# One core, attention and routed experts: the end of the first attention in another order

## What is computed

```python
x = x + attn_a(layernorm(x))     # qkv, windows of 64 with 16 heads of 8, projection,
                                 # + residual; layer norm, 128->512 GELU, 512->128, + residual
x = x + ffn(layernorm(x))        # router: top 2 of 8 experts; silu(x W1[e]) W2[e], gated
x = x + attn_b(layernorm(x))     # overlapping windows of 128, one softmax over all 128 features
x = x + ffn(layernorm(x))
```

## Time and profile before

| | |
|---|---|
| median of 3 runs | 621.07 us (612.94 to 622.57) |
| profiled execution | 618.1 us, span 616.2 us |
| mean granted PE clock | 0.881 of full speed |
| PE busy | 476.2 us, 77% of the span |
| DVE busy | 314.9 us, 51% |
| POOL busy | 251.7 us, 41% |
| ACT busy | 233.3 us, 38% |
| chain that ended last | PE 64%, DVE 15%, issue 8%, DMA 5%, POOL 3%, ACT 2% |

### The profile page before, as it was taken

How to read it: one execution, slowest core, us unless ns; L and a number is a source line. 1 busy time by engine, 2 the same in 40 slices (tenths; PEclk the granted TensorE clock), 3 DMA queues, 4 the chain that set the end, 5 groups by cost and what they waited for, 6 DMA issues and landing times.

```text
span 616.2 us, 12385 instructions
## 1 busy us (share of the span) xinstructions
PE 476.2 (77%) x3973; PEld 375.2 (61%) x3995; DVE 314.9 (51%) x1032; ACT 233.3 (38%) x483; POOL 251.7 (41%) x233
## 2 busy tenths in 40 slices
PE   1839999999989999766977999138776399599940
PEld 1525676867767786736867777116565287577730
DVE  5545586858876897745401010086977442010105
ACT  6715556474546447041321222114542022122320
POOL 7033343334342654435173533421265607533440
PEclk9957899999989999867997999658996589799985
DMA  7581092873748180012113200220010311320006
GB/s 256 184 186 31 20 192 60 155 155 64 161 72 158 34 173 14 14 35 70 33 57 86 69 15 27 64 90 1 0 36 26 75 41 50 87 66 31 24 23 204
DMA packets 66401, 48.35 MB, mean 78 GB/s; under 512 B 7669, under 2 KB 60423, under 8 KB 66342
## 3 DMA queue, kind: packets, MB, share of 16 engines
q1 hardware_dynamic: 61238, 36.99, 27.1%
q0 software_dynamic: 5104, 10.57, 4.8%
HBM read 16.14 MB, written 27.59 MB: 71 GB/s over the span
## 4 chain that ended last, share of the span: by engine, by line
PE 64%; DVE 15%; issue 8%; DMA 5%; POOL 3%; ACT 2%; SPq 2%; POOLq 0%; DVEq 0%; ACTq 0%
PE PS L796 12%; PE PS L656 8%; PE PS L780 7%; PE PS L782 4%; PE PS L643 3%; PE PS L781 3%; PE PS L701 3%; PE PS L618 3%; PE PS L600 3%; PE PS L708 2%; PE PS L559 2%; DVE X L1678 2%; PE PS L759 2%; PE PS L666 2%; PE PS L627 2%
## 5 line engine op out<-in xcount | busy, mean ns | idle before, releaser
L497 POOL DMA_INDIRECT YY<-W2R,ID x78 | 76.4, 980 | 85.7 <-ACT W2R L1230 65.6
L441 POOL TENSOR_TENSOR R<-NM,I64B 128x1024 bf16<-128x1024 f32 x32 | 61.5, 1922 | 112.9 <-DVE NM L1371 107.9
L1222 ACT ACTIVATE W2R<-PS 128x512 f32<-128x512 f32 x78 | 46.6, 597 | 160.4 <-PE PS L782 160.3
L796 PE MATMUL PS<-WB,W2R 128*128 x624 | 92.5, 295 | 0.0
L1638 DVE COPY QKM<-PS 128x1024 bf16<-128x1024 bf16 (+1 forms) x20 | 13.6, 678 | 148.0 <-PE PS L759 148.0
L483 POOL DMA_INDIRECT XS<-W1R,SLOT x64 | 63.4, 990 | 57.8 <-PE PS L782 33.4
L780 PE MATMUL PS<-QKM,WA 128*128 128x128 bf16 x312 | 71.7, 234 | 12.1 <-DVE QKM L1638 4.5
L796 PEld LDWEIGHTS PS<-WB,W2R 128*128 128x128 f32 x624 | 79.7, 200 | 1.7 <-issue 0.2
L782 PE MATMUL PS<-QKM,WA 128*128 128x128 bf16 x312 | 71.8, 234 | 0.0
L781 PE MATMUL PS<-QKM,WA 128*128 128x128 bf16 x312 | 69.7, 227 | 0.0
L656 PEld LDWEIGHTS PS<-VB,PF 128*128 128x128 f32 x512 | 59.6, 191 | 6.3 <-issue 6.3
(11 more groups left out here) (197 smaller groups left out, 864.9 us busy)
## 6 DMA issues: line engine op xcount, KB each, us to landing
XS<-CST SPq DMA_DIRECT2D x30, 520.0 KB, 9.1
QKM<-XS SPq DMA_DIRECT2D x78, 65.0 KB
QKM<-QK SPq DMA_DIRECT2D x64, 72.0 KB, 2.1
QKM<-YY SPq DMA_DIRECT2D x8, 512.0 KB, 5.7
W2R<-in_W POOLq DMA_DIRECT2D x1, 2048.0 KB, 11.5
YY<-W2R,ID POOLq DMA_INDIRECT x78, 2.2
XS<-CST SPq DMA_DIRECT2D x2, 585.0 KB, 9.2
XS<-W1R,SLOT POOLq DMA_INDIRECT x64, 2.4
```

What stands on the lines that cost most here:

```text
L441: nc.gpsimd.tensor_tensor(R[:, u % 2], NM[:, u % 2].unsqueeze(2).to_broadcast([P, NH, WIN]), I64B[:].unsqueeze(1).to_broadcast([P, NH, WIN ...
L497: pool.indirect_dma_start(out=YY[f], out_offset=to, in_=YS[n % NY][:, i, :], in_offset=None, bounds_check=NPAIRS - 1, oob_is_err=False) \
L796: last = mm(o, HF[n % 3][:, k, :], WB[:, e, k, :].rearrange("p o c -> p (o c)"), start=k == 0, stop=k == KF - 1)
L1222: fn(HF[n % 3], PS[:, n % 3, :].rearrange("p (k s) -> p k s", k=KF), ACT.Silu).then_inc(s["f_hf"], 1)
```

## The change

At the end of the first attention the order on every engine is another. The last unit of attention (context 31) is freed of `output_a(2)` and of the first table. Then come, on PE, `project(3)`, `output_a(2)`, `h_t(3)`, the four hidden matmuls of batch 3 in four banks (5, 0, 1, 2), a new `output_a_by_quarter(3)`, which takes each hidden quarter as its GELU is done, and only then `route_x_t(0, 2)` and `logits(0, 2)`. Batch 1's logits, choice, ranks and place move up into units 28 to 30. Batch 2's choice, ranks, place and table move into the first two expert tiles; in the first expert layer batch 3's transposes, logits and ranks move from t = 2, 3, 6 to t = 4, 5, 8. On POOL, batch 1's dispatches move ahead of batch 3's power, and batch 3's eight dispatches stand in one block between the first and the second send of YY. The residual of batch 3 is kept in XN.

```diff
...
-                if c >= 3:
-                    dispatch(0, c - 3, (t,))
+                if c == B - 1:
+                    dispatch(0, 0, (t,))
+                if c == B - 1 and t == 7:
+                    dispatch(0, 1, (0,))
...
             def dispatch(f, c, parts=range(TOP_K * TB)):
...
             def send_back(f):
                 for y, tiles in enumerate(YGROUPS):
...
-                    if y < 2:
+                    if f == 0 and y == 1:
+                        dispatch(f, B - 1)
+                    if f == 1 and y < 2:
                         for i in range(4 * y, 4 * y + 4):
...
-            for t in range(4):
-                beside(B, t)
-            pool.wait_ge(s["a_proj_ps"], B)
-            for t in range(4, 8):
-                beside(B, t)
+            biases_a(B - 1)
+            dispatch(0, 1, range(1, 8))
+            rstd(0, "h", B, o=NT)
+            rstd(0, "f", B - 1, o=NT + TB)
...
-            pool.wait_ge(s["a_y_ps"], B)
+            rstd(0, "f", B, o=NT + TB)
...
-            rstd(0, "f", B, o=NT + TB)
...
             def b_bias(b):
...
-        XT_BANK = ((7, 7, 7, 3), (2, 2, 2, 3))
-        LG = [(7, 0), (7, 0), (7, 0), (3, 0)], [(3, 0)] * 4
-        RK = [(5, 0), (5, 0), (5, 0), (3, 0)], [(3, 0)] * 4
+        XT_BANK = ((7, 7, 3, 3), (2, 2, 2, 3))
+        LG = [(7, 0), (7, 0), (3, 0), (3, 0)], [(3, 0)] * 4
+        RK = [(5, 0), (7, 0), (3, 0), (3, 0)], [(3, 0)] * 4
+        MLP_BANK = [(5, 7, 5, 7)] * (B - 1) + [(5, 0, 1, 2)]
+        ROUTED = ((4, 5, 8), (2, 3, 6))
...
-                if b == B - 1:
-                    pe.wait_ge(s["f_rk"], B - 2)
+                if b:
+                    pe.wait_ge(s["a_h1"], FA * b)
                 for j in range(TB):
...
-                if f == 1 and b:
-                    pe.wait_ge(s["f_lg"], b)
-                if f >= 2:
+                if f == 1 and b == 1:
+                    pe.wait_ge(s["f_lg"], 1)
+                if f == 1 and b == 2:
+                    pe.wait_ge(s["f_rk"], 2)
+                if f == 1 and b == B - 1:
+                    pe.wait_ge(s["a_nm"], B * NU * 2)
+                    pe.wait_ge(s["a_pf"], B * NU * 2)
+                if f >= 2 and b < B - 1:
...
-                mm(PS[:, 5 + 2 * (f % 2), :], W1A[:, f * P:f * P + P], HT[:], start=True, stop=True).then_inc(s["a_h_ps"], 1)
+                mm(PS[:, MLP_BANK[b][f], :], W1A[:, f * P:f * P + P], HT[:], start=True, stop=True).then_inc(s["a_h_ps"], 1)
...
             def output_a(b):
...
+                last.then_inc(s["a_y_ps"], 1)
+
+            def output_a_by_quarter(b):
+
+                pe.wait_ge(s["a_res2"], b)
+                for k in range(FA):
+                    pe.wait_ge(s["a_h1"], b * FA + k + 1)
+                    for j in range(TB):
+                        last = mm(PS[:, 7, j * D:j * D + D], H1[:, k, j * P:j * P + P], W2A[:, k, :],
+                                  start=k == 0 and j == 0, stop=k == FA - 1 and j == TB - 1, skip_group_check=True)
...
             def route_x_t(f, c):
...
                 def routed(t):
...
-                    if t == 2:
+                    if f == 0 and t == 1:
+                        ranks(f, c - 1)
+                    if t == ROUTED[f][0]:
...
-                    if t == 3:
+                    if t == ROUTED[f][1]:
...
-                    if t == 6:
+                    if t == ROUTED[f][2]:
...
             def between(c, t):
...
-                if t == 0 and c >= 3:
-                    pe.wait_ge(s["a_h1"], FA * (c - 2) + 3)
-                    ranks(0, c - 3)
+                if t == 0 and c == B - 1:
+                    pe.wait_ge(s["a_h1"], FA + 3)
+                    ranks(0, 0)
+                if t == 6 and c == B - 1:
+                    ranks(0, 1)
                 if t == 1 and 1 <= c < B:
...
-                if t == 0 and c >= 2:
+                if t == 0 and 2 <= c < B:
...
-                if t == 5 and c >= 2:
-                    if c + 1 < B:
-                        pe.wait_ge(s["a_sel"], 10 * (c + 1) + 4)
-                    logits(0, c - 2)
+                if t == 4 and c == B - 1:
+                    logits(0, 1)
+                if t == 5 and c == 2:
+                    pe.wait_ge(s["a_sel"], 10 * (c + 1) + 4)
+                    logits(0, 0)
                 if t == 5 and c == 0:
...
-            for t in range(3, 8):
-                between(B, t)
-                beside(B, t)
-            between(B + 1, 0)
-            output_a(B - 1)
+            project(B - 1)
+            output_a(B - 2)
+            h_t(B - 1)
+            for k in range(FA):
+                hidden_a(B - 1, k)
+            output_a_by_quarter(B - 1)
+            route_x_t(0, B - 2)
+            logits(0, B - 2)
...
             def at(w):
...
             def gelu(b, k):
...
-                fn(H1[:, k, :], PS[:, 5 + 2 * (k % 2), :], ACT.Gelu, bias=B1A[:, k:k + 1]).then_inc(s["a_h1"], 1)
+                fn(H1[:, k, :], PS[:, MLP_BANK[b][k], :], ACT.Gelu, bias=B1A[:, k:k + 1]).then_inc(s["a_h1"], 1)
...
             def route_x_t(f, c):
...
-            for t in range(3, 8):
-                between(B, t)
-                beside(B, t)
+            h_t(B - 1)
+            for k in range(FA):
+                gelu(B - 1, k)
+            route_x_t(0, B - 2)
...
             def experts(f):
                 def silu(t):
...
-                    if t == 2:
+                    if t == ROUTED[f][0]:
...
-            res = lambda j: RES2[:, j, :]
+            RES = [RES2] * (B - 1) + [XN]
...
             def residual(b):
...
-                st.did(v.tensor_tensor(RES2[:], PS[:, 5, :].rearrange("p (j d) -> p j d", d=D), XN[:], ALU.add))
+                st.did(v.tensor_tensor(RES[b][:], PS[:, 5, :].rearrange("p (j d) -> p j d", d=D), XN[:], ALU.add))
...
-                variance(st, res, "h_var", o=NT)
+                variance(st, lambda j: RES[b][:, j, :], "h_var", o=NT)
...
             def residual_normalised(b):
...
-                normalise(HZ, res, 0, "a_hz", o=NT)
+                normalise(HZ, lambda j: RES[b][:, j, :], 0, "a_hz", o=NT)
...
             def output_a(b):
...
-                v.tensor_tensor(RES2[:], PS[:, 7, :].rearrange("p (j d) -> p j d", d=D), RES2[:], ALU.add) \
+                v.tensor_tensor(RES[b][:], PS[:, 7, :].rearrange("p (j d) -> p j d", d=D), RES[b][:], ALU.add) \
...
-                v.tensor_tensor(xs, xs, RES2[:], ALU.add).then_inc(s["a_x"], 1)
+                v.tensor_tensor(xs, xs, RES[b][:], ALU.add).then_inc(s["a_x"], 1)
...
-                if t == 0 and c >= 3:
-                    route_place(0, c - 3)
+                if t == 0 and c == B - 1:
+                    route_place(0, 0)
                 if t == 1 and c + 1 < B:
...
-                if t == 1 and c >= 2:
+                if t == 1 and 2 <= c < B:
...
-                if t == 1 and c == B:
-                    route_table(0, 0)
-                if t == 2 and c >= 2:
+                if t == 2 and 2 <= c < B:
...
-                if t == 6 and c >= 2:
-                    route_choose(0, c - 2)
+                if t == 5 and c == B - 1:
+                    route_choose(0, 1)
+                if t == 6 and c == B - 1:
+                    route_place(0, 1)
+                if t == 6 and c == 2:
+                    route_choose(0, 0)
                 if t == 7 and c + 2 < B:
...
-            for t in range(3, 8):
-                beside(B, t)
-            route_place(0, B - 2)
-            route_table(0, 1)
+            route_table(0, 0)
+            residual(B - 1)
+            residual_normalised(B - 1)
+            output_a(B - 2)
+            dve.wait_ge(s["a_x"], B - 1)
+            route_variance(0, B - 2)
+            route_normalised(0, B - 2)
+            route_split(0, B - 2)
...
-                route_variance(f, c)
-                turned(0)
-                identities(0)
+                if f == 0:
+                    turned(0)
+                    route_choose(f, c - 1)
+                    identities(0)
+                    route_place(f, c - 1)
+                    route_table(f, 1)
+                    route_variance(f, c)
+                else:
+                    route_variance(f, c)
+                    turned(0)
+                    identities(0)
...
```

## The result

| | before | changed |
|---|---|---|
| median with the first result | 617.73 us (4 runs) | 626.35 us (4 runs), ratio 1.0143, 95% interval 1.0088 to 1.0198 |
| median in the experiments' first round | 616.75 us (25 runs) | 623.61 us (8 runs), ratio 1.0076, interval 1.0026 to 1.0126 |
| profiled execution, first | 618.1 us, span 616.2 | 626.67 us, span 624.8 |
| span of a second profile | 614.7 | 621.2 |
| mean granted PE clock, two profiles | 0.881, 0.883 | 0.862, 0.868 |

The first row has one execution of the kernel before more than the three of its table above. The ratios are taken from the executions in the faster of the kernel's two states alone, so they are not the quotients of the medians. The change makes the kernel about 1% slower, 7 to 8.6 us by the medians.

A forecast was written before the change was run, and what follows sets the result against it. Bounds: a PE, DVE and POOL relay ending attention, then batch 3's dispatches gating the experts' third phase. Attention's 4.0 to 8.9 us gain against 6.5 to 7.2 lost gave -2.4 to +3.2, taken as -1: 618.6 us, range 611 to 626.

The forecast's parts named there:

- O: End of output_a(3) on PE, before the experts; 280.37 us before, forecast at 271.5 to 276.4.
- the choice in unit 29: Batch 1's early choice on DVE delays PE's ranks and later work by 2.6 us; bounds 0 and 4.1.
- The last unit: Context 31 without output_a(2), residual add and table: project(3) starts at 255.8 instead of 257.85, -2.0 us.
- project(3) to O: Tail of attention: transposes start 2.7 to 1.0 us sooner relative to project(3); the rest saves 4.1 to 0.9.
- From O to the third phase: From the last output_a to the experts' tiles 16 to 38: 52.8 to 53.5 us against 46.26, +6.5 to +7.2.
- The hole at group 2: PE waits about 6 us before the experts' third group of transposes, for batch 2's late rows.
- Rival C: Slower: routing chain as sized, small lead, low tail clock, choice stretched 1.5 us; +3.2 to +4.7 us, chance 0.23.
- the lead: How much sooner attention's last output_a ends than before: 4.0 to 8.9 us.
- A: Forecast case, 0.50: attention ends 6 to 9 us sooner, a new expert hole takes it back; -2.4 to +1.
- the lean to the fast clock: Matmuls in attention's tail expected nearer full speed, as the longest hole there would be some 1.5 us.
- the sum's fast end: Whole kernel with a fast PE clock: -8.9 + 6.5 = -2.4 us.
- The slow end of every step: Whole kernel with a slow PE clock: -4.0 + 7.2 = +3.2 us.

The follow-up runs named there:

- x9: Changed kernel with batch 1's ranks moved from the head to the end of unit 30; ratio 1.0060 to the kernel before.
- x3: Kernel before with only batch 3's eight dispatches in one block, ahead of the first send of YY; ratio 0.9876, median 610.0 us.
- b2: Kernel before, unchanged, profiled a second time; span 614.7 us.
- x7: Kernel before with batch 3's dispatches in one block ahead of the sends, four MLP banks and output by quarter; ratio 0.9859, median 608.77 us.
- x8: Changed kernel with batch 1's routing back, batch 3's ranks ahead of the third group's transposes, its dispatch block before the first send; ratio 0.9968 to before.
- x2: Changed kernel with batch 1's logits, choice, ranks, place and dispatches back in their old places; ratio 1.0082 to the kernel before.
- x6: Changed kernel with PE's output_a(2) back in the last attention unit, DVE's part staying late; ratio 1.0171 to the kernel before.
- a2: Changed kernel, unaltered, measured and profiled a second time; ratio 1.0076 to the kernel before.
- x5: Changed kernel with batch 3's eight dispatches mixed with the first two sends of YY as before; ratio 1.0158 to the kernel before.
- x1: Changed kernel with batch 3's ranks in the first experts ahead of the third group's transposes; ratio 1.0023 to the kernel before.

## Why the prediction was wrong, step by step

**Up to O, the choice in unit 29: mechanism partly right, too small.** Forecast +2.6 us, from R28 to weighted(30). In the two pairs of the account it was +5.2 (26.6 and 29.2 against 22.0 and 23.5). Over all profiles, R28 to weighted(30) is 22.0, 23.5, 22.0, 28.4, 23.6 and 23.5 us where batch 1's routing stands in its old place, mean 23.8; it is 26.6, 29.2, 25.9, 25.9, 29.2, 26.6 and 26.6 where it is early with ranks at the unit's head, mean 27.1: +3.3. Where PE waited at ranks, in four of these seven, the wait was 2.2 us; beyond what the choice holds up on DVE (x9) the time went into matmuls at the low clock. Low clock was found with early routing in all seven; without it there was none in two of six profiles, 3.4 us of it in three (it cost 1.5 us each) and 13.7 us in one (x3). So it isn't the early routing's own. In the four with the wait it set in within 0.6 us behind it. In b2, x7 and x8, and in the three early ones without the wait, it set in 1.0 to 1.9 us behind the start of batch 1's logits, in x3 0.4 us behind it, with PE busy up to then. That the narrow matmuls there call it is only argued: no run left them out, and in two profiles (before, x2) they ran without it. What calls the low clock in the loop stays open.

**The last unit: the step that failed.** I had it, from weighted(30)'s start to project(3), at 7.8 us (247.98 to 255.8) for 12.5 before. It was 10.7 and 10.9 in the changed kernel. With output_a(2) gone PE has only a context to do while DVE divides. My sum had that division, 1.4 us, and not the hole that it makes on PE: it priced weighted(31) at the 1.9 us of the high level and gave the short holes as the reason for a fast clock. The hole is 1.93 us, and behind it weighted(31) takes 3.35 and 3.60 us instead of 1.9, each context 1.1 instead of 0.6. That is some 2 us of the 2.9 and 3.1 that were missing. The other 1.0 is the division: one step of it took 1.04 us for 0.18, beside POOL's biases. I had put the biases' queue on POOL in the sum and not their effect on DVE. weighted(31) was slow, 2.4 to 3.6 us, in all eight profiles with this hole, and fast, 1.87, in all six without it: five of the old order, and x6, which differs from the changed kernel in that place alone. So the slow matmuls come with the missing output_a(2); that the hole's length is what lowers the clock is not shown, since in a2 PE stopped at 252.57 and the clock fell at 252.8.

**project(3) to O: within bounds.** Forecast 15.7 to 20.6 us (22.5 before), measured 19.25 and 17.57. project(3) took 3.78 us, a little over my upper end, and 3.3 to 3.8 in all fourteen profiles, so the 1.8 us of my lower end never came. HZ's transposes to O took 10.5 and 8.8, between my ends of 8.7 and 11.9. Batch 1's seven dispatches were off the path, as worked out.

**From O to the third phase: right.** +6.5 to +7.2 forecast, +6.8 measured. The hole at group 2 (6 us forecast, 5.98 and 7.07 measured), the ranks behind it, and the 5.2 us that the block gives back (x3, x5) each came out nearly as sized. In x1, with the ranks' place alone mended, nothing of the +6.8 is left (46.7 us, for 46.4 before).

**The sum.** Rival C came nearest: slower when the lead is under 6.5 us. The lead is 0.5 us in the two pairs of profiles from R28 on, where I had 4.0 to 8.9. C had only part of the mechanism, and its price of +3.2 to +4.7 was too low: the choice that it had stretched took 2.64 us on DVE, unstretched, and its clock was low in the tail only. The 0.50 given to A and the lean to the fast clock were the mistake: the rows of before showed project(3) slow after a hole, and I read the end of the new order at the high clock because its holes were shorter. From R28 on the pairs differ by +6.3, 8.7 more than the -2.4 of the sum's fast end: 3.0 are the last unit, 2.6 the choice, 2.8 project(3) to O, 0.3 the part behind O. The slow end of every step gave +3.2, and with the failed step's 3.0 that comes to the measured +6.3 or nearly, but this is luck: the choice was 2.6 short there as well, and project(3) to O 2.1 quicker than its slow end.

The Trainium skill (TensorE: Matmul & The Clock Gate, Part 1) says that the monitor which sets the clock runs free of the kernel, so how many matmuls are slow varies. The runs agree: the same attention code ran from R28 to weighted(30) in 22.0 and in 28.4 us (before, x3). Those 6.4 us between two single profiles are as much as the largest effect sized here, so the small ones, up to O above all, are known only roughly.

## What to carry to other kernels

When work that covered a wait is moved away, price the work behind the new hole at the low clock as well; here a hole of 1.9 to 2.5 us was followed by slow matmuls in eight profiles of eight. In an in-order queue a short step that starts a long chain (ranks, slots, eight dispatches, loads) belongs ahead of any wait it doesn't need: that place was worth 6 us here, more than all that the reordering won. And try the parts of a reordering singly: one of them alone (the block of dispatches, in its strongest form) is 1.2% faster than before, while the whole was 1% slower.

## What the runs showed of the hardware

A DVE operation with two SBUF operands took 1.81 us (`route_place`'s product at 239.57); 0.22 is the median of that line's eight instances. It started behind POOL's multiply, 239.41 to 241.30, and ended with it. The Trainium skill (SBUF — State Buffer, SBUF: two separate sides) describes such a port shared by the two and held for a whole instruction; the trace agrees. Indirect dispatches kept their pace: in trains of eight, one started 1.26 to 1.35 us behind the other, and batch 1's seven of the changed kernel, 256.31 to 263.91, by 1.26 to 1.29, with DVE busy for 0.90 us of 263 to 264.
